# A graph-attention layer on one core: x loaded in 8 transfers of 128 partitions, four more adjacency pieces masked in halves

## The chip, the cores and the metric

One core of one Trainium2 chip runs the whole program. The metric is the device time of one execution in microseconds (us). TensorE multiplies matrices (PE; its weight loads are PEld), VectorE is DVE, ScalarE is ACT, GpSimd is POOL, and SyncE (SP) only issues transfers. ACT issues transfers too, in line with its own instructions. All transfers run on the core's 16 DMA engines.

## The reference

N = 4096 nodes with D = 128 features and a dense 4096 x 4096 int32 adjacency (67.1 MB; x is 2.1 MB):

```
s_i = emb @ attn[:d]
s_j = emb @ attn[d:]
e = leaky_relu(s_i + s_j.T, negative_slope=0.2)
e = e + where(adj > 0, 0.0, neg_inf)
alpha = softmax(e, axis=1)
x = layernorm(x + alpha @ emb, axis=-1)
```

## The kernel before

The rows are cut into 8 blocks of 512 (BLOCKS) and the columns into 4 pieces of 1024 (PIECES), which makes 32 adjacency pieces of 2 MB. ORDER interleaves the first two blocks and then goes block by block. Below, piece g is the g-th of this order; "pieces 5 to 8" are g = 5 to 8 with counting from 0. A piece is 8 chunks of 128 columns.

**Start.** SP loads the attention row (one row of 1 KB). Then x comes in three parts (X_CUTS): chunks 0 to 7, 8 to 15 and 16 to 31. Each part is four transfers, one for each quadrant of 32 partitions; SP issues the two low quadrants, ACT the two high ones. In the same queues the adjacency follows: pieces 0 and 1 by half rows (load_rows, 256 KB a transfer), the later ones by quadrants (load_piece, 512 KB). PE transposes x (turn_x), ACT copies the result out of PSUM (L407), PE multiplies it with the first half of attn for the row scores (s_i_piece, L884). DVE multiplies x with the second half (product_of, L611) and sums over features (sum_products, L607); ACT sums one of the four stripes (L416). DVE takes the largest s_j (L647, row_max_ready), PE spreads it over the partitions (L900), DVE reduces it again (L649), and exponentials of the scores follow on ACT (L421 to L428). Only then can the first weights be made. ACT's program has, in this order: its x loads, four transfers of piece 0, the copy of x tile 0, two transfers of piece 1, tiles 1 and 2, two more, tiles 3 and 4, L416, one transfer of piece 2, tiles 5 to 7, another, and then the exponentials.

**Steady state.** For each piece ACT turns the int32 adjacency into bytes: in halves for g in HALVED (half_to_bytes, L451, two instructions), else at once (to_bytes, L457). DVE transposes the bytes by 32 x 32 blocks into mask_t: in halves (turn_half, L679) or whole (turn, L666). It then makes one weight tile a chunk (weigh, L771), 8 a piece. PE accumulates xj times weights (block_product, L919, two passes a chunk); after each block it transposes the sums back (L913), and the last block goes the other way round (L924). DVE's program places the transpose of the next piece (or of its first half) after chunk TURN_AT = 5, or after chunk 7 for the pieces in LATE_TURNS; the second half of a halved piece is transposed after its chunk 3. At chunk 3 of pieces 9 and 10, DVE also does the residual of blocks 0 and 1.

Instructions of one engine run in the order of its program; there is no scheduler.

Of the kernel before, what the change touches and what calls it, by code (L numbers as in the profile page):

```python
# [14 lines left out]
def gat_kernel(nc: bass.Bass, x: bass.AP, adj: bass.AP, attn: bass.AP, out: bass.AP):  # L15
# [8 lines left out]
    P = 128  # L24
    N, D = x.shape
    DEN = D - 1
    Q = 4
    B = 32
    K = 4
    F = N // (Q * B * K)  # L30
# [21 lines left out]
    W_SLOTS = 12  # L52
    BY_DVE = 1
    SECOND_HALF_AT = 3
    HALVED = (0, 1, 2, 3, 4)
    TURN_AT = 5
    LATE_TURN_AT = PC - 1
    TURN_BACK_AT = 6
# [11 lines left out]
    BY_POOL = range(1, PC)  # L70
    SPLIT = (0, 1)
    ROWS_HALF = (slice(0, Q // 2), slice(Q // 2, Q))
    LATE_TURNS = (0, 1, 2)
    SLOPE = 0.2
    EPS = 1e-5
    NEG_INF = -1e9
# [11 lines left out]
    BACK_BANK = [1, 0]  # L88
    X_CUTS = [0, SC, 2 * SC, CHUNKS]
    X_PARTS = len(X_CUTS) - 1  # L90
    IN_FLIGHT = 3
    WARM = 14

    adj_v = adj.rearrange("(r f b k) (q u c) -> f u q b k r c", r=Q, f=F, b=B, k=K, q=Q, u=PIECES)
    x_v = x.rearrange("(q f b k) d -> q b f (k d)", q=Q, f=F, b=B, k=K)
    out_v = out.rearrange("(q f b k) d -> f q b (k d)", q=Q, f=F, b=B, k=K)
    xi_v = x.rearrange("(t p) d -> p t d", p=P)

    with ExitStack() as ctx:
# [156 lines left out]

            return x_raw[:, t, :]

        def load_x(queue, quadrants, part):

            first, stop = X_CUTS[part], X_CUTS[part + 1]
            for q in quadrants:
                queue.dma_start(x_raw[B * q:B * (q + 1), first:stop, :].rearrange("b (f k) d -> b f (k d)", k=K),  # L263
                                x_v[q, :, first // K:stop // K, :]).then_inc(x_loaded[part], 16)

        def load_piece(queue, quadrants, g):

# [43 lines left out]
        @block.sync  # L311
        def _(sp):

            sp.dma_start(attn_row_in[:], attn[:, :].rearrange("d o -> o d")).then_inc(attn_loaded, 16)
            for part in range(X_PARTS):
                load_x(sp, LOW_HALF, part)
            for g in SPLIT:
                for h in range(2):
                    load_rows(sp, LOW_HALF, g, h)
            for g in range(len(SPLIT), ALL_PIECES):  # L320
                load_piece(sp, LOW_HALF, g)


            for g in range(EARLY):
                sp.wait_ge(early_out_ready, g + 1)
                for q in LOW_HALF:
                    store_last(sp, g, q, last_stored)
            for g in range(EARLY, len(FINAL_GROUPS)):
                sp.wait_ge(last_out_ready, g - EARLY + 1)
                for q in LOW_HALF:  # L330
                    store_last(sp, g, q, last_stored)


            sp.wait_ge(again_ready, 1)
            with sp.If(sp.value_load(again[0:1, 0:1], min_val=0, max_val=1) > 0):
                sp.wait_ge(stored, 16 * Q * NORM_GROUPS)
                sp.wait_ge(early_stored, 16 * len(HIGH_HALF) * EARLY)
                sp.wait_ge(last_stored, 16 * (Q * len(FINAL_GROUPS) - len(HIGH_HALF) * EARLY))
                sp.dma_start(xi[:], xi_v).then_inc(inputs_again, 16)
                sp.dma_start(attn_col, attn[D:2 * D, :]).then_inc(inputs_again, 16)  # L340
                sp.dma_start(attn_row, attn[0:D, :].rearrange("d o -> o d").broadcast_to([P, D])).then_inc(inputs_again, 16)
                with sp.Fori(0, TILES) as t:
                    sp.wait_ge(adj_rows_free, t + 1)
                    sp.dma_start(adj_rows, adj[bass.ds(t * P, P), :]).then_inc(adj_rows_loaded, 16)
            sp.wait_ge(early_stored, 16 * len(HIGH_HALF) * EARLY)
            sp.wait_ge(last_stored, 16 * (Q * len(FINAL_GROUPS) - len(HIGH_HALF) * EARLY))
# [51 lines left out]
        @block.scalar  # L398
        def _(act):

            for part in range(X_PARTS):
                load_x(act, HIGH_HALF, part)
            for h in range(2):
                load_rows(act, HIGH_HALF, 0, h)
            for m in range(RB):
# [196 lines left out]
        def _(dve):  # L602
# [11 lines left out]
            def first_quarter(h):  # L614

                part = slice(0, P)
                nc.vector.tensor_scalar(mask_bytes[:, 0, :, ROWS_HALF[h], part], split_rows(0, h)[:, :, :, part], 0.0, None,  # L617
                                        ALU.is_gt).then_inc(half_bytes_ready, 1)
                dve.wait_ge(half_bytes_ready, h + 1)
                src = mask_bytes[:, 0, :, ROWS_HALF[h], part].bitcast(u32)  # L620
                dst = mask_t[:, 0, 0, :, :].rearrange("p i k -> p (i k)").bitcast(u32)
# [7 lines left out]
            dve.wait_ge(attn_i_in_psum, 1)  # L629
            nc.vector.tensor_copy(attn_iw[:], banks[ATTN_I_BANK][:, 0:P]).then_inc(attn_wide, 1)  # L630
            dve.wait_ge(attn_j_ready, 1)
            dve.wait_ge(x_loaded[0], 16 * Q)
            product_of(0)
            sum_products(0)
            dve.wait_ge(x_loaded[1], 16 * Q)
            product_of(1)
            sum_products(1)
            dve.wait_ge(x_loaded[2], 16 * Q)
            product_of(2)
            product_of(3)  # L640
            sum_products(3)
# [3 lines left out]
            dve.wait_ge(s_j_ready, STRIPES - 1)  # L645
            dve.wait_ge(s_j_by_act_ready, 1)
            nc.vector.reduce_max(smax[:, 0:1], s_j[:], X).then_inc(row_max_ready, 1)  # L647
            dve.wait_ge(max_spread, 1)
            nc.vector.reduce_max(smax[:, 1:2], banks[MAX_BANK][:, 0:P], X).then_inc(max_found, 1)  # L649
            dve.wait_ge(max_found, 1)  # L650
# [1 line left out]
            nc.vector.tensor_scalar(smax[:, 2:3], smax[:, 1:2], SLOPE - 1, None, ALU.mult).then_inc(max_scaled, 1)  # L652
            dve.wait_ge(adj_loaded[0], 16 * Q)
            first_quarter(1)

            def turn(g):

# [197 lines left out]
        def _(pe):  # L855
# [10 lines left out]
            def turn_x(m):  # L866

                if m * K in X_CUTS:
                    pe.wait_ge(x_loaded[X_CUTS.index(m * K)], 16 * Q)
                if m >= 4:  # L870
                    pe.wait_ge(xT_ready, m - 3)
                for k in range(K):
# [162 lines left out]
```

## Time and profile before

| | us |
|---|---|
| median of 3 runs (252.03 to 252.84) | 252.11 |
| the profiled execution | 252.82 |
| its span on the core | 251.0 |
| PE busy | 240.3 |
| DVE busy | 234.0 |
| ACT busy | 173.6 |

The profiled execution is 0.71 us above the median, and 1.8 us of it lie outside the span. PE's granted clock was full over the whole span. A busy PE means that a matmul was in flight: passes of 128x512 start every 0.43 us when nothing holds them.

### The profile page before, as it was taken

How to read it: one execution, taken by the hardware profiler on the slowest of the kernel's cores; microseconds unless marked ns; L12 is line 12 of the kernel's file. 1: busy time of each engine (PE TensorE's matmuls, PEld its weight loads, DVE VectorE, ACT ScalarE, POOL GpSimd, SP SyncE). 2: the span in 40 equal slices, each digit the busy share in tenths (PEclk: the TensorE clock that was granted, in tenths of full speed). 3: DMA queues.
4: the chain of work that ended last, by engine and by line, in shares of the span. 5: the costliest groups of instructions: out<-in, count | busy, mean ns of one | idle time of the engine just before them, and what ended most of it. 6: DMA issues, size and time to landing. Idle time of an engine off the chain costs nothing.

```text
span 251.0 us, 2790 instructions
## 1 busy us (share of the span) xinstructions
PE 240.3 (96%) x801; PEld 126.3 (50%) x801; DVE 234.0 (93%) x385; ACT 173.6 (69%) x253; POOL 42.9 (17%) x81
## 2 busy tenths in 40 slices
PE   7789999989999999999999999999999999999991
PEld 6444444334444444444444444444444444799991
DVE  1989999989999999999999999999999999999834
ACT  0688768889887696996996669686976559404402
POOL 1029000000000024430430003300330004300612
PEclk9999999999999999999999999999999999999999
DMA  7999999999999999999999999999999990100001
GB/s 198 299 346 347 350 348 347 348 347 347 347 347 349 345 349 348 336 359 351 347 349 363 347 348 347 347 363 347 350 347 363 347 281 3 44 0 1 24 21 45
DMA packets 70386, 71.50 MB, mean 285 GB/s; under 512 B 3009, under 2 KB 68866, under 8 KB 70370
## 3 DMA queue, kind: packets, MB, share of 16 engines
q1 hardware_dynamic: 34754, 34.74, 44.2%
q10 hardware_dynamic: 34656, 34.67, 43.9%
q0 software_dynamic: 960, 1.90, 2.4%
q8 instruction: 7, 0.11, 0.2%
q14 instruction: 9, 0.07, 0.1%
HBM read 69.21 MB, written 2.10 MB: 284 GB/s over the span
## 4 chain that ended last, share of the span: by engine, by line
PE 77%; DMA 14%; DVE 3%; ACT 2%; issue 1%; SPq 1%; ACTq 0%
PE psum L919 64%; PE psum L924 11%; DMA adj_in<-in_adj_dram 11%; DMA x_raw<-in_x_dram 3%; ACT mask_bytes L457 1%; PE psum L913 1%; DVE adj_in L611 1%; SPq L263 1%; ACT mask_bytes L446 1%; DVE s_j L607 0%; DVE weights L771 0%; DVE mask_bytes L617 0%; ACTq L282 0%; PE psum L900 0%; ACT q_row L428 0%
## 5 line engine op out<-in xcount | busy, mean ns | idle before, releaser
L919 PE MATMUL psum<-weights,xj 128*128 128x512 f32 x448 | 193.9, 593 | 1.5 <-DVE weights L771 1.5
L771 DVE SCALAR_TENSOR_TENSOR weights<-q_row,r_j,mask_t 128x512 f32<-128x512 f32 x256 | 172.5, 741 | 0.5
L919 PEld LDWEIGHTS psum<-weights,xj 128*128 128x128 f32 x448 | 84.5, 190 | 106.5 <-issue 82.2
L457 ACT ACTIVATE mask_bytes<-adj_in 128x4096 uint8<-128x4096 int32 x27 | 97.5, 3613 | 26.3 <-DMA adj_in<-in_adj_dram 22.6
L666 DVE STREAM_TRANSPOSE mask_t<-mask_bytes 128x1024 uint32<-128x1024 uint32 x27 | 33.4, 1236 | 1.0 <-ACT mask_bytes L457 1.0
L924 PEld LDWEIGHTS psum<-xj,weights 128*128 128x128 f32 x256 | 28.8, 192 | 0.5 <-issue 0.5
L924 PE MATMUL psum<-xj,weights 128*128 128x128 f32 x256 | 28.9, 275 | 0.0
L371 POOL TENSOR_SCALAR neg_mean<-total 128x4 f32<-128x4 f32 x7 | 2.1, 295 | 148.4 <-ACT x_raw L470 148.3
L380 POOL DMA_DIRECT2D out_dram<-x_raw x28 | 14.6, 527 | 19.7 <-ACT x_raw L484 19.6
L470 ACT ACTIVATE x_raw<-x_raw 128x128 f32<-128x128 f32 x28 | 8.2, 294 | 11.2 <-DVE x_raw L714 11.2
L451 ACT ACTIVATE mask_bytes<-adj_in 128x2048 uint8<-128x2048 int32 x6 | 11.1, 1902 | 4.4 <-DMA adj_in<-in_adj_dram 4.4
L477 ACT ACTIVATE unused<-x_raw,neg_mean 128x128 f32<-128x128 f32 x28 | 10.9, 390 | 4.3 <-POOL neg_mean L371 4.3
L484 ACT ACTIVATE x_raw<-x_raw,offset,rstd 128x128 f32<-128x128 f32 x28 | 11.5, 480 | 2.6 <-POOL offset L377 2.6
L434 ACT ACTIVATE xj<-x_raw,last_x,d_j 128x127 f32<-128x127 f32 x25 | 10.3, 479 | 0.0
L375 POOL TENSOR_TENSOR rstd<-variance,half 128x4 f32<-128x4 f32 x7 | 9.6, 1369 | 0.6
L714 DVE SCALAR_TENSOR_TENSOR x_raw<-psum,rden,x_raw 128x127 f32<-128x127 f32 x32 | 9.2, 344 | 0.4
L465 ACT COPY sums<-psum 128x512 f32<-128x512 f32 x7 | 4.1, 582 | 6.2 <-PE psum L919 6.2
L884 PE MATMUL psum<-adj_in,attn_iw 128*128 128x512 f32 x16 | 7.6, 597 | 0.4 <-ACT adj_in L407 0.4
L365 POOL TENSOR_SCALAR xj<-x_raw,d_j,last_x 128x127 f32<-128x127 f32 x7 | 7.0, 1010 | 0.1
L679 DVE STREAM_TRANSPOSE mask_t<-mask_bytes 128x512 uint32<-128x512 uint32 x9 | 6.3, 704 | 0.5 <-ACT mask_bytes L451 0.5
L446 ACT ACTIVATE mask_bytes<-adj_in 128x1024 uint8<-128x1024 int32 x6 | 5.9, 1046 | 1.2 <-DMA adj_in<-in_adj_dram 1.0
L554 ACT ACTIVATE deviations<-moments,eps 128x1 f32<-128x1 f32 x2 | 0.6, 295 | 8.4 <-DVE moments L738 8.4
(68 smaller groups left out, 85.0 us busy)
## 6 DMA issues: line engine op xcount, KB each, us to landing
adj_in<-in_adj_dram SPq DMA_DIRECT2D x60, 512.0 KB, 13.9
adj_in<-in_adj_dram ACTq DMA_DIRECT2D x60, 512.0 KB, 14.0
adj_in<-in_adj_dram ACTq DMA_DIRECT2D x8, 256.0 KB, 10.6
adj_in<-in_adj_dram SPq DMA_DIRECT2D x8, 256.0 KB, 11.2
out_dram<-x_raw POOLq DMA_DIRECT2D x28, 64.0 KB, 5.3
x_raw<-in_x_dram ACTq DMA_DIRECT2D x4, 128.0 KB, 3.4
x_raw<-in_x_dram SPq DMA_DIRECT2D x4, 128.0 KB, 3.7
x_raw<-in_x_dram ACTq DMA_DIRECT2D x2, 256.0 KB, 6.1
```

The source lines that it names most:

```text
L375: nc.gpsimd.tensor_tensor(rstd[:, 0:K], variance[:, 0:K], half[:, 0:K], ALU.pow).then_inc(rstd_ready, 1)
L380: pool.dma_start(out_v[g, q, :, :], x_raw[B * q:B * (q + 1), g * K:(g + 1) * K, :].rearrange("b k d -> b (k d)")).then_inc(stored, 16)
L434: nc.scalar.activation(xj[:, c, 0:DEN], x_raw[:, c, 0:DEN], ACT.Identity, bias=last_x[:, c:c + 1], scale=d_j[:, c:c + 1]).then_inc(xj_scal ...
L451: half_bytes = nc.scalar.activation(mask_bytes[:, g % BYTE_SLOTS, :, :, part], adj_in[:, g % ADJ_SLOTS, :, :, part], ACT.Sign)
L457: nc.scalar.activation(mask_bytes[:, g % BYTE_SLOTS, :, :, :], adj_in[:, g % ADJ_SLOTS, :, :, :], ACT.Sign).then_inc(bytes_ready, 1)
L477: last = nc.scalar.activation(unused[:, k, :], tile(g * K + k), ACT.Square, bias=neg_mean[:, k:k + 1], accum_out=square_sum[:, k:k + 1])
L484: last = nc.scalar.activation(tile(g * K + k), tile(g * K + k), ACT.Identity, bias=offset[:, k:k + 1], scale=rstd[:, k:k + 1])
L666: nc.vector.transpose(dst.rearrange("p f (r a) -> p r f a", a=B), src).then_inc(mask_ready, 1)
L714: nc.vector.scalar_tensor_tensor(features, sums_of(n, t)[:, 0:DEN], rden[:, t:t + 1], features, ALU.mult, ALU.add).then_inc(y_ready, 1)
L771: nc.vector.scalar_tensor_tensor(weights[:, slot_of(g * PC + j), :], q_row[:, n * BANK:(n + 1) * BANK], r_j[:, c:c + 1], mask_t[:, g % MAS ...
L919: nc.tensor.matmul(banks[SUM_BANK[n % 2]][:, :], xj[:, c, :], weights[:, slot_of(g * PC + j), :], start=(c == 0), stop=(c == CHUNKS - 1)). ...
L924: return nc.tensor.matmul(banks[((BLOCKS - 1) * K + t) % 8][:, 0:D], weights[:, slot, t * P:(t + 1) * P], xj[:, c, :], start=(c == 0), sto ...
```

## The change

x comes in 8 transfers of 256 KB. Transfer f takes chunks 4f to 4f + 3 of all 128 partitions, one run of 2 KB for each partition; SP issues the odd f and ACT the even ones. In DRAM the rows of one f lie in four groups of 32 rows, one group for each quadrant, 512 KB apart: the new x_v has dimensions f, q (4), b (32), 512 elements. Part 0 of x is now two transfers, part 1 two, part 2 four (LOADS). HALVED takes in pieces 5 to 8, LATE_TURNS takes in piece 3, and the transposes of piece 0's first quarter come out of first_quarter into turn_first_quarter, the first of them behind the largest s_j.

```diff
-    HALVED = (0, 1, 2, 3, 4)
+    HALVED = tuple(range(9))
-    LATE_TURNS = (0, 1, 2)
+    LATE_TURNS = (0, 1, 2, 3)
+    LOADS = [(stop - first) // K for first, stop in zip(X_CUTS, X_CUTS[1:])]
-    x_v = x.rearrange("(q f b k) d -> q b f (k d)", q=Q, f=F, b=B, k=K)
+    x_v = x.rearrange("(q f b k) d -> f q b (k d)", q=Q, f=F, b=B, k=K)
-        def load_x(queue, quadrants, part):
-
-            first, stop = X_CUTS[part], X_CUTS[part + 1]
-            for q in quadrants:
-                queue.dma_start(x_raw[B * q:B * (q + 1), first:stop, :].rearrange("b (f k) d -> b f (k d)", k=K),
-                                x_v[q, :, first // K:stop // K, :]).then_inc(x_loaded[part], 16)
+        def load_x(queue, f):
+
+            part = max(i for i in range(X_PARTS) if X_CUTS[i] <= f * K)
+            queue.dma_start(x_raw[:, f * K:(f + 1) * K, :].rearrange("p k d -> p (k d)"),
+                            x_v[f, :, :, :]).then_inc(x_loaded[part], 16)
...
-            for part in range(X_PARTS):
-                load_x(sp, LOW_HALF, part)
+            for f in range(1, F, 2):
+                load_x(sp, f)
...
-            for part in range(X_PARTS):
-                load_x(act, HIGH_HALF, part)
+            for f in range(0, F, 2):
+                load_x(act, f)
...
+
+            def turn_first_quarter(h):
+
+                part = slice(0, P)
                 dve.wait_ge(half_bytes_ready, h + 1)
...
-            dve.wait_ge(x_loaded[0], 16 * Q)
+            dve.wait_ge(x_loaded[0], 16 * LOADS[0])
...
             nc.vector.reduce_max(smax[:, 0:1], s_j[:], X).then_inc(row_max_ready, 1)
+            turn_first_quarter(0)
...
             first_quarter(1)
+            turn_first_quarter(1)
```

The first place is the head of SP's program; the sizes are those of the SBUF side (partitions, runs, elements of a run). On ACT the x rows change in the same way.

```order
 L311 UNCONDITIONAL_BRANCH
 L314 DMA attn_row_in<-in_L_gnn_attn_dram 1x256
-L263 DMA x_raw<-in_x_dram 32x2x512 x4
-L263 DMA x_raw<-in_x_dram 32x4x512 x2
+L263 DMA x_raw<-in_x_dram 128x1x512 x4
 L293 DMA adj_in<-in_adj_dram 32x8x256 x8
 L282 DMA adj_in<-in_adj_dram 32x16x256 x60
```

Six transfers became four on each queue, and the SBUF side of each now has 128 partitions with one run.

The second place is on DVE between the sums over features and the first weights; first before, then with the change.

```order
L607 TENSOR_REDUCE s_j<-adj_in 128x8
L617 TENSOR_SCALAR mask_bytes<-adj_in 128x4x2x128
L622 STREAM_TRANSPOSE mask_t<-mask_bytes 128x4x64
L647 TENSOR_REDUCE smax<-s_j 128x1
L649 TENSOR_REDUCE smax<-psum 128x1
L651 TENSOR_SCALAR below_max<-s_j,smax 128x32
```

```order
L607 TENSOR_REDUCE s_j<-adj_in 128x8
L617 TENSOR_SCALAR mask_bytes<-adj_in 128x4x2x128
L651 TENSOR_REDUCE smax<-s_j 128x1
L626 STREAM_TRANSPOSE mask_t<-mask_bytes 128x4x64
L654 TENSOR_REDUCE smax<-psum 128x1
L656 TENSOR_SCALAR below_max<-s_j,smax 128x32
```

One transpose moved behind the first of the two reductions to the largest s_j. Lines of the change are 4 to 6 higher.

The third place is on DVE from the weights of piece 3 (its second half) into piece 5; first before, then with the change.

```order
L771 SCALAR_TENSOR_TENSOR weights<-q_row,r_j,mask_t 128x512 x2
L679 STREAM_TRANSPOSE mask_t<-mask_bytes 128x512
L771 SCALAR_TENSOR_TENSOR weights<-q_row,r_j,mask_t 128x512 x6
L679 STREAM_TRANSPOSE mask_t<-mask_bytes 128x512
L771 SCALAR_TENSOR_TENSOR weights<-q_row,r_j,mask_t 128x512 x2
L666 STREAM_TRANSPOSE mask_t<-mask_bytes 128x16x2x32
L771 SCALAR_TENSOR_TENSOR weights<-q_row,r_j,mask_t 128x512 x8
```

```order
L777 SCALAR_TENSOR_TENSOR weights<-q_row,r_j,mask_t 128x512 x4
L685 STREAM_TRANSPOSE mask_t<-mask_bytes 128x512
L777 SCALAR_TENSOR_TENSOR weights<-q_row,r_j,mask_t 128x512 x4
L685 STREAM_TRANSPOSE mask_t<-mask_bytes 128x512
L777 SCALAR_TENSOR_TENSOR weights<-q_row,r_j,mask_t 128x512 x2
L685 STREAM_TRANSPOSE mask_t<-mask_bytes 128x512
L777 SCALAR_TENSOR_TENSOR weights<-q_row,r_j,mask_t 128x512 x6
L685 STREAM_TRANSPOSE mask_t<-mask_bytes 128x512
```

The first half of piece 4 is transposed two weights later, and piece 5 is transposed in two halves instead of at once.

## Rows read from the trace of the kernel before

**Rows 1.** The chain that ended last: start us, us, what.

```profile
3.41 7.58 DMA x_raw<-in_x_dram
...
83.61 27.47 PE psum L919 x64
```

**Rows 2.** Timeline of PE's products: start us, us, instructions, idle before.

```profile
19.59 25.91 PE L919 MATMUL psum<-weights,xj 128*128 128x512 f32 x60
45.85 7.13 PE L919 MATMUL psum<-weights,xj 128*128 128x512 f32 x16 [0.35 <-DVE weights L771]
54.17 16.12 PE L919 MATMUL psum<-weights,xj 128*128 128x512 f32 x37 [1.18 <-DVE weights L771]
```

**Rows 3.** Timeline of DVE at the start.

```profile
11.01 2.36 DVE L611 TENSOR_TENSOR adj_in<-x_raw,attn_j 128x1024 f32<-128x1024 f32 x2 [0.51 <-DMA x_raw<-in_x_dram]
...
15.26 0.45 DVE L622 STREAM_TRANSPOSE mask_t<-mask_bytes 128x256 uint32<-128x256 uint32 x1
...
17.07 0.69 DVE L617 TENSOR_SCALAR mask_bytes<-adj_in 128x1024 uint8<-128x1024 int32 x1
...
18.36 2.96 DVE L771 SCALAR_TENSOR_TENSOR weights<-q_row,r_j,mask_t 128x512 f32<-128x512 f32 x4
```

**Rows 4.** DMA issues: line, queue, count, KB each, median us from issue to landing.

```profile
x_raw<-in_x_dram ACTq DMA_DIRECT2D x4, 128.0 KB, 3.4
x_raw<-in_x_dram SPq DMA_DIRECT2D x4, 128.0 KB, 3.7
x_raw<-in_x_dram ACTq DMA_DIRECT2D x2, 256.0 KB, 6.1
x_raw<-in_x_dram SPq DMA_DIRECT2D x2, 256.0 KB, 6.9
...
attn_row_in<-in_L_gnn_attn_dram SPq DMA_DIRECT2D x1, 1.0 KB
```

**Rows 5.** Stretches; after the engines: granted clock, share of 16 DMA engines, GB/s.

```profile
2.00:9.00 7.00, 5.81 (x34) 4.90 (x34) 3.75 (x5) 2.30 (x4) 0.00 (x0) 1.00 1.02 278
...
20.00:24.00 4.00, 4.00 (x11) 1.81 (x10) 3.96 (x6) 3.01 (x4) 4.00 (x5) 1.00 1.10 348
```

**Rows 6.** The page's GB/s in 40 slices of 6.3 us.

```profile
GB/s 198 299 346 347 350 348 347 348 347 347 347 347 349 345 349 348 336 359 351 347 349 363 347 348 347 347 363 347 350 347 363 347 281 3 44 0 1 24 21 45
```

**Rows 7.** Issues of transfers: timeline, then piece 0 and 1's, ns min/median/max.

```profile
0.73 2.80 ACTq L263 DMA_DIRECT2D x_raw<-in_x_dram  x6
1.14 2.70 SPq L263 DMA_DIRECT2D x_raw<-in_x_dram  x6
...
L293 SPq DMA_DIRECT2D adj_in<-in_adj_dram x8: 622/738/1861, 3.9 to 10.2; - x8
```

**Rows 8.** Timeline of ACT at the start.

```profile
13.91 1.32 ACTq L282 DMA_DIRECT2D adj_in<-in_adj_dram  x1
...
14.63 1.52 ACT L407 COPY adj_in<-psum 128x512 f32<-128x512 f32 x3
...
16.96 0.23 ACT L421 ACTIVATE d_j<-below_max 128x32 f32<-128x32 f32 x1 [0.81 <-DVE below_max L651]
```

**Rows 9.** Timeline of DVE from 25 us on.

```profile
25.50 2.74 DVE L771 SCALAR_TENSOR_TENSOR weights<-q_row,r_j,mask_t 128x512 f32<-128x512 f32 x4
...
32.29 2.74 DVE L771 SCALAR_TENSOR_TENSOR weights<-q_row,r_j,mask_t 128x512 f32<-128x512 f32 x4
...
44.45 0.71 DVE L679 STREAM_TRANSPOSE mask_t<-mask_bytes 128x512 uint32<-128x512 uint32 x1 [0.48 <-ACT mask_bytes L451]
...
52.14 1.25 DVE L666 STREAM_TRANSPOSE mask_t<-mask_bytes 128x1024 uint32<-128x1024 uint32 x1 [0.96 <-ACT mask_bytes L457]
53.31 5.35 DVE L771 SCALAR_TENSOR_TENSOR weights<-q_row,r_j,mask_t 128x512 f32<-128x512 f32 x8
...
59.74 5.35 DVE L771 SCALAR_TENSOR_TENSOR weights<-q_row,r_j,mask_t 128x512 f32<-128x512 f32 x8
...
94.89 5.35 DVE L771 SCALAR_TENSOR_TENSOR weights<-q_row,r_j,mask_t 128x512 f32<-128x512 f32 x8
```

More of the change, by code:

```diff
@@ L631, in _ @@
             dve.wait_ge(attn_j_ready, 1)
-            dve.wait_ge(x_loaded[0], 16 * Q)
+            dve.wait_ge(x_loaded[0], 16 * LOADS[0])
             product_of(0)
             sum_products(0)
-            dve.wait_ge(x_loaded[1], 16 * Q)
+            dve.wait_ge(x_loaded[1], 16 * LOADS[1])
             product_of(1)
             sum_products(1)
-            dve.wait_ge(x_loaded[2], 16 * Q)
+            dve.wait_ge(x_loaded[2], 16 * LOADS[2])
             product_of(2)
@@ L868, in turn_x @@
                 if m * K in X_CUTS:
-                    pe.wait_ge(x_loaded[X_CUTS.index(m * K)], 16 * Q)
+                    pe.wait_ge(x_loaded[X_CUTS.index(m * K)], 16 * LOADS[X_CUTS.index(m * K)])
                 if m >= 4:
```

## The prediction

> **What bounds the kernel now.** I read the chain that ended last first. It starts with the transfer of x, which lands at 10.99 us, goes through DVE's products, and from there to the end is nearly all PE products [rows 1]. So I asked where PE itself stands still. Its products begin at 19.59 us and run at 27.47 / 64 = 0.429 us a pass [rows 1, 2]. The profile finds only two stops of PE after that, 0.35 and 1.18 us, both for DVE's weights [rows 2]. Whatever is to be gained or lost must therefore be a shift of 19.59, or those 1.5 us.
>
> Next the start. DVE's program is a chain of products and sums; x holds it up for only 0.51 us, at the last two stripes [rows 3]. The first weights begin at 18.36, right behind piece 0's second byte half (17.07 + 0.69) and its transpose [rows 3]. In the steady state the 16 DMA engines are full and deliver 348 GB/s [rows 5], so pieces of 2 MB come every 6.0 us, while PE takes 16 x 0.429 = 6.87 us for one. The adjacency is needed at its own pace only in the first pieces.
>
> **Part 1: x in 8 transfers.** Fewer issues save sequencer time only: two issues less on each queue at 2.80 / 6 = 0.47 us [rows 7], hidden because the engines are already full from 2 us on (share 1.02) [rows 5]. What matters is how a transfer is dealt to the 16 engines. All x and adjacency transfers of before have 32 rows outermost on the SBUF side and 32 or 128 on the DRAM side, and they fill all 16 engines [rows 5]. The one transfer with a single row, that of attn, is the only one in the view of issues without a time to landing [rows 4]: it did not end in 16 parts. So the number of parts follows the pattern. In the new transfer the SBUF side has 128 rows, but the DRAM side is 4 groups of 32 rows, since a quadrant's rows lie 512 KB from the next quadrant's, and no row of before shows such a shape. If the dealing goes by the outermost loop of both sides, only 4 of the 16 engines carry x. If it goes by runs or by SBUF rows, all 16 do.
>
> I take the first. Nothing in the rows shows the DRAM side of a transfer being cut below its outermost loop, and the outermost loops of before are all multiples of 16 except the one that shows no landing. The Trainium skill (DMA: Bandwidth & Descriptors, "Why a DMA increments its semaphore by 16 and not by 1") states this as a rule: the engines used are the largest number up to 16 that divides the slowest dimension, other than 1, of both patterns; here that is the largest divisor of 4 and 128, so 4. The attn row agrees with it, and no run here shows a 4 yet.
>
> The price: x is 2048 KB [rows 4], so each of the 4 engines carries 524,288 bytes. The highest rate that the page shows is 363 GB/s [rows 6], 22.7 GB/s for each engine, which gives 23.1 us. While x loads today the rate is 278 GB/s [rows 5], 17.4 per engine, which gives 30.2 us; that is the slow bound, with all 16 in each other's way. An engine whose neighbours are idle may go faster than 22.7, since that figure is shared among 16; I allow a tenth (an estimate) and get 20.8 us as the fast bound. I take 23.1, nearest to four engines alone. Traffic is full from 2.0 us [rows 5], so the last of x lands at 25.1 instead of 10.99: **+14.1 us**. The first adjacency pieces are queued behind x on these 4 engines, and a piece is complete only with all of its parts: piece 0 follows 131,072 / 22.7 = 5.8 us after x, at 30.9, where it came 6.1 us after x before (17.07). So adjacency moves with x, and at 5.8 to 6.0 us a piece it then keeps the pace it had.
>
> The Trainium skill also gives about 27 GiB/s for one engine (same page, "Specifications"). By it x would take 18.1 us and the whole sum be 5.0 us lower; no row here shows such a rate.
>
> **What the full queue does to ACT.** The issue of a 256 KB adjacency transfer takes 0.6 to 0.75 us at first and 1.86 at most [rows 7]: by 8 us the queues are full. SP had then issued 1 MB of x and 1.6 MB of adjacency, and half of 278 GB/s x 6.3 us, 0.9 MB, had left its queue: about 1.7 MB or some 105 runs of 1 KB for each engine is what a queue holds. With x on 4 engines a queue carries 4 x 32 = 128 runs on each of them, full as soon as x is issued. Each adjacency transfer then needs 16 free places, and gets them only as the 4 engines clear x, two queues sharing them: 16 x 2048 / 11.35 = 2.9 us. ACT issues eight of these among its copies of tiles 0 to 2, 8 x 2.9 = 23 us from about 2.6, so it reaches tile 3 at 25.8, 0.7 us after x. Then two transfers of piece 2 with 32 runs of 1 KB each, also 2.9 us apiece, stand between L416 and the exponentials, where today they take 0.6 and 1.3 us [rows 8]. Today the last copies end at 14.63 + 1.52 = 16.15, 5.2 us after x, and the exponentials start at 16.96, 6.0 after x [rows 8]. Late by 0.7 to 1.8 us, these partly hide behind PE's eight score passes, which end at 19.6, 8.6 after x.
>
> **Part 2: the transpose behind the largest s_j.** It takes 0.45 us [rows 3] out of the way of row_max_ready and lies then under PE's spread of the maximum. Worth at most 0.45, and nothing where DVE waits for piece 0 anyway. The delay on ACT and this gain go together: between -0.45 and +1.4; I take **+0.3**.
>
> **Part 3: halves for pieces 5 to 8, late turn of piece 4.** The late turn comes two weights (1.4 us) later than where DVE stands 0.48 us for ACT's bytes [rows 9]: that wait goes. The wait of 0.96 at piece 5 [rows 9] is for a whole L457 of 3.6 us; half of it is ready 1.7 us sooner, so it goes too. PE's two stops of 1.53 us end with them. But a halved piece costs DVE 32.29 - 25.50 = 6.79 us, a whole one 59.74 - 53.31 = 6.43 [rows 9]: 4 x 0.36 = 1.44 us more. DVE is hardly faster than PE's 6.87 in that stretch, so its lead must carry this until pieces 9 and 10 with their residuals. Today the weights for chunk 0 of piece 11, the third of the row at 94.89, end at 94.89 + 3 x 0.67 = 96.9 [rows 9], and PE takes them at 83.61 + 17 x 0.858 = 98.2 [rows 1]: lead 1.3. In the tight stretch the lead is (19.59 + 8 x 0.858) - (25.50 + 0.69) = 0.26 [rows 2, 9], and PE runs without a stop on it. DVE saves 1.44 of waits and pays 1.44 of halves, so PE can gain no more than the spare lead, 1.3 - 0.26, here rounded down: **-0.9 us** (bounds 0 and -1.5).
>
> **Sum.** 252.82 (the profiled execution) + 14.1 + 0.3 - 0.9 = 266.3; that execution is 0.71 above the median of 252.11, so 265.6 against the median. I say 265.5.
>
> **Rivals.** (a) *Same mechanism, slower*: x on 4 engines at today's 17.4 GB/s lands at 32.2, 21.2 later than now: 252.1 + 21.2 + 0.3 - 0.9 = 272.7, and 274.7 with ACT's blocked issues at their bound of 1.4 and nothing from part 3. Against it speaks that the rate of today is one that 16 engines share.
>
> (b) *Faster*: x is dealt to all 16 engines, by its 128 SBUF rows. Then x lands no later than now, and the start gains at most DVE's wait of 0.51 [rows 3], while DVE's first weights still wait for piece 0 at 17.07, whose bytes are no sooner there. What is left is part 3: 252.1 - 0.9 = 251.2 (250.7 to 251.7). For it speaks that today's transfers, whose runs are also 2 KB, fill all engines; against it, that none of them has fewer than 32 in its outermost loop. The point that decides is the number of engines: 14 or more at 17.4 GB/s bring x by 11 us. The Trainium skill ("Rules for kernel authors", same page) speaks for this side in advising one transfer of 128 partitions over two of half of them; its rule above has the condition that this shape fails.
>
> (c) *No change*: as (b), but DVE's 1.44 us of halves eat the lead up to piece 11 and PE stops there instead of at pieces 3 and 5: 252.1.
>
> **Chances.** Forecast (x on 4 engines, 261 to 269) 0.67; (a) 0.17; (b) 0.11; (c) 0.05. A change within 0.3%, 0.75 us, can't be told from none here. Slower 0.84, same 0.05, faster 0.11. The case of 4 engines has its own range: fast bound 252.1 + 14.1 - 2.3 - 0.45 - 1.5 = 261.9, slow bound 274.7; I give 261 to 274. The cases (b) and (c), 0.16, stay outside.
>
> **What would show it.** The x rows of the issues lose their time to landing, as attn's has none. The share of the DMA engines falls well under 1 in the first 20 us. DVE's last products (L611) start at about 25 instead of 11.01, PE's first product at about 34. SP's and ACT's issues of pieces 0 and 1 take about 2.9 us each. PE's stops at pieces 3 and 5 are gone, and the lead at piece 11 is near 0.3. The prediction is wrong if x lands at 11 us or before; then (b) or (c) holds.

## The result and the profile after

| | us | ratio to the kernel before (95% interval) |
|---|---|---|
| kernel before, median of 6 runs | 252.16 | |
| changed kernel, median of 6 runs (374.36 to 379.25) | 377.47 | 1.495 (1.4911 to 1.4989) |
| forecast | 265.5 (261 to 274) | 1.053 |

Slower was right, and the size was not: 125 us instead of 13. The profiled execution took 374.36 us, with a span of 372.6 where the one of before had 251.0: 121.6 us to find.

The chain of the changed kernel that ended last (start us, us, what) answers to [rows 1].

```profile
3.52 29.29 DMA x_raw<-in_x_dram
...
37.54 24.07 DMA adj_in<-in_adj_dram
...
61.63 0.02 ACT mask_bytes L451
...
61.69 18.68 DMA adj_in<-in_adj_dram
...
80.46 19.16 DMA adj_in<-in_adj_dram
...
329.30 3.62 ACT mask_bytes L457
...
342.74 24.53 PE psum L930 x200
```

It begins, as forecast, with a late x: 3.52 + 29.29 = 32.81 us instead of 10.99. But then it does not become PE's products. It is adjacency, transfer after transfer, up to 329 us. Each link is about 19 us and carries the chain on by two pieces.

The page of the changed kernel: the GB/s in 40 slices (9.3 us each), the count of packets, the chain by engine, one group of instructions, and the issues of x.

```profile
GB/s 69 176 157 212 224 220 213 216 216 217 216 216 217 217 216 216 216 217 226 236 215 213 216 254 215 216 217 236 242 212 217 252 239 218 225 90 28 1 30 30
DMA packets 70226, 71.50 MB, mean 192 GB/s; under 512 B 2849, under 2 KB 68706, under 8 KB 70210
...
DMA 86%; PE 7%; ACT 4%; issue 1%; ACTq 1%; DVE 1%; POOL 0%
...
L457 ACT ACTIVATE mask_bytes<-adj_in 128x4096 uint8<-128x4096 int32 x23 | 83.2, 3617 | 101.5 <-DMA adj_in<-in_adj_dram 101.5
...
x_raw<-in_x_dram ACTq DMA_DIRECT2D x4, 256.0 KB
x_raw<-in_x_dram SPq DMA_DIRECT2D x4, 256.0 KB
```

The slices that read 336 to 363 in [rows 6], mostly near 348, read 212 to 254 here, mostly near 216, from the fourth slice to the end of the adjacency. ACT stands 101.5 us waiting for it ahead of L457. The x rows have lost the time to landing that they had in [rows 4]. I read this as for the attn row: the transfer doesn't end in 16 parts. The pages' counts of small packets bear it out, if each part ends with one. Under 512 B the page of before counts 3009 packets and this one 2849: 160 fewer, and 12 x 16 - 8 x 4 is 160.

Stretches of the changed kernel (length; busy time and instructions of PE, PEld, DVE, ACT, POOL; granted clock, DMA share, GB/s), beside [rows 5]. The last row is the kernel before in the same 100 us.

```profile
5.00:10.00 5.00, 0.93 (x4) 0.63 (x3) 0.58 (x2) 0.00 (x0) 0.00 (x0) 1.00 0.26 102
10.00:20.00 10.00, 3.55 (x16) 3.14 (x16) 4.01 (x4) 0.25 (x1) 0.00 (x0) 1.00 0.65 170
...
60.00:160.00 100.00, 80.90 (x173) 33.12 (x172) 68.32 (x109) 53.90 (x62) 2.17 (x4) 0.93 1.11 216
...
60.00:160.00 100.00, 100.00 (x246) 45.08 (x246) 99.72 (x161) 79.80 (x106) 16.84 (x30) 1.00 1.10 349
```

Two things are to be seen. While x loads, the share is 0.26, which is 4.2 of 16 engines, and these move 102 GB/s. From 60 us on the engines are busy all the time (1.11, before: 1.10) and yet move only 216 GB/s, where the kernel before has 349. A full share alone is no proof of a full rate.

The timelines of PE and of DVE in the changed kernel, beside [rows 2] and [rows 3].

```profile
44.24 7.12 PE L925 MATMUL psum<-weights,xj 128*128 128x512 f32 x16 [2.20 <-issue]
54.33 10.17 PE L925 MATMUL psum<-weights,xj 128*128 128x512 f32 x16 [2.97 <-DVE weights L777]
65.22 4.96 PE L925 MATMUL psum<-weights,xj 128*128 128x512 f32 x11 [0.72 <-DVE weights L777]
```

```profile
32.83 2.36 DVE L611 TENSOR_TENSOR adj_in<-x_raw,attn_j 128x1024 f32<-128x1024 f32 x2 [11.95 <-DMA x_raw<-in_x_dram]
...
42.01 0.79 DVE L617 TENSOR_SCALAR mask_bytes<-adj_in 128x1024 uint8<-128x1024 int32 x1 [2.74 <-DMA adj_in<-in_adj_dram]
```

**Where the 121.6 us are.** Before, PE came to piece 2 at 19.59 + 2 x 6.87 = 33.3 us [rows 1, 2]; now at 65.22: 31.9 late. From piece 2 (bytes at 61.63) to piece 30 (329.30) a piece takes (329.30 - 61.63) / 28 = 9.56 us instead of PE's 6.87: 28 x 2.69 = 75.3 more. The remainder, 14.4, is behind the last pieces, whose bytes, sums and normalization no longer lie under PE's products. So not quite a fifth is x (21.8 us at its landing), and most of the rest is the rate of the adjacency; with that rate restored, in e11 below, the time is 269.28 us.

### The profile page after: what moved, and what is told of

The parts are those of the page before. It is cut to its first block, busy times and chain, and to the rows that moved or that the text cites. A ratio compares the mean times of both kernels' runs of the same rounds, so it can differ in the third digit from the quotient of the medians.

```text
span 372.6 us, 2795 instructions
## 1 busy us (share of the span) xinstructions
PE 275.1 (74%) x801; PEld 138.9 (37%) x801; DVE 238.6 (64%) x389; ACT 174.5 (47%) x257; POOL 37.5 (10%) x81
## 2 busy tenths in 40 slices
DMA packets 70226, 71.50 MB, mean 192 GB/s; under 512 B 2849, under 2 KB 68706, under 8 KB 70210
## 3 DMA queue, kind: packets, MB, share of 16 engines
q10 hardware_dynamic: 34576, 34.67, 46.9%
## 4 chain that ended last, share of the span: by engine, by line
DMA 86%; PE 7%; ACT 4%; issue 1%; ACTq 1%; DVE 1%; POOL 0%
DMA adj_in<-in_adj_dram 78%; DMA x_raw<-in_x_dram 8%; PE psum L930 7%; ACT mask_bytes L457 2%; ACTq L263 1%; ACT adj_in L416 1%; ACT x_raw L484 0%; ACT unused L477 0%; ACT adj_in L407 0%; ACT x_raw L470 0%; PE psum L879 0%; PE psum L919 0%; ACT sums L465 0%; DVE x_raw L752 0%; DVE x_raw L720 0%
## 5 line engine op out<-in xcount | busy, mean ns | idle before, releaser
L925 PE MATMUL psum<-weights,xj 128*128 128x512 f32 x448 | 216.8, 641 | 36.5 <-DVE weights L777 34.2
L925 PEld LDWEIGHTS psum<-weights,xj 128*128 128x128 f32 x448 | 89.7, 206 | 158.3 <-issue 98.1
L457 ACT ACTIVATE mask_bytes<-adj_in 128x4096 uint8<-128x4096 int32 x23 | 83.2, 3617 | 101.5 <-DMA adj_in<-in_adj_dram 101.5
L672 DVE STREAM_TRANSPOSE mask_t<-mask_bytes 128x1024 uint32<-128x1024 uint32 x23 | 28.6, 1244 | 50.4 <-ACT mask_bytes L457 50.4
L451 ACT ACTIVATE mask_bytes<-adj_in 128x2048 uint8<-128x2048 int32 x14 | 26.0, 1903 | 30.7 <-DMA adj_in<-in_adj_dram 30.7
L919 PE MATMUL psum<-ident,sums 128*128 128x128 f32 x28 | 7.2, 408 | 35.5 <-ACT sums L465 35.5
L685 DVE STREAM_TRANSPOSE mask_t<-mask_bytes 128x512 uint32<-128x512 uint32 x17 | 12.0, 708 | 25.0 <-ACT mask_bytes L451 21.8
L919 PEld LDWEIGHTS psum<-ident,sums 128*128 128x128 f32 x28 | 5.0, 208 | 41.4 <-ACT sums L465 39.8
L611 DVE TENSOR_TENSOR adj_in<-x_raw,attn_j 128x1024 f32<-128x1024 f32 x4 | 4.8, 1224 | 21.6 <-DMA x_raw<-in_x_dram 21.6
L879 PE MATMUL psum<-ident,x_raw 128*128 128x128 f32 x32 | 7.1, 394 | 13.1 <-DMA x_raw<-in_x_dram 13.1
L879 PEld LDWEIGHTS psum<-ident,x_raw 128*128 128x128 f32 x32 | 5.9, 210 | 16.5 <-DMA x_raw<-in_x_dram 15.3
```

The source lines that it names most:

```text
L451: half_bytes = nc.scalar.activation(mask_bytes[:, g % BYTE_SLOTS, :, :, part], adj_in[:, g % ADJ_SLOTS, :, :, part], ACT.Sign)
L457: nc.scalar.activation(mask_bytes[:, g % BYTE_SLOTS, :, :, :], adj_in[:, g % ADJ_SLOTS, :, :, :], ACT.Sign).then_inc(bytes_ready, 1)
L672: nc.vector.transpose(dst.rearrange("p f (r a) -> p r f a", a=B), src).then_inc(mask_ready, 1)
L685: nc.vector.transpose(dst.rearrange("p (r a) -> p r a", a=B), src).then_inc(mask_ready if f else half_mask_ready, 1)
L879: last = nc.tensor.transpose(banks[XT_BANK + m % 4][:, k * P:(k + 1) * P], x_raw[:, m * K + k, :], ident[:])
L919: last = nc.tensor.transpose(banks[BACK_BANK[n % 2]][:, t * P:(t + 1) * P], sums[:, t * P:(t + 1) * P], ident[:])
```

## The experiments

The theory that I formed from these rows, P: (1) x goes over 4 engines, because the DRAM side has 4 groups outermost; (2) these four fall behind the other twelve, and with that the two queues fall out of step; (3) SP's queue writes only partitions 0 to 63 and ACT's only 64 to 127, and transfers into one half of the partitions reach some 217 GB/s. The rivals: the four engines' lag costs the rate by itself; part 3 or the order of DVE does it; the DRAM side is what is shared.

One thing has to be kept in mind throughout. A quadrant of the partitions always receives the same quarter of the adjacency's columns (q stands for both in adj_v). So "one half" below means 64 partitions and, in DRAM, the half of the columns that goes into them.

**e1: of the change only x; e2: all but x.**

e1 is the kernel before with this, e2 the changed kernel without it:

```diff
+    LOADS = [(stop - first) // K for first, stop in zip(X_CUTS, X_CUTS[1:])]
-    x_v = x.rearrange("(q f b k) d -> q b f (k d)", q=Q, f=F, b=B, k=K)
+    x_v = x.rearrange("(q f b k) d -> f q b (k d)", q=Q, f=F, b=B, k=K)
...
-                load_x(sp, LOW_HALF, part)
+            for f in range(1, F, 2):
+                load_x(sp, f)
...
```

> The kernel before with the x loads of the change and nothing else. Theory A (the x transfers alone cost the 125 us; the halves and the moved transposes are worth about a microsecond): 373 to 381 us, x landing near 33 us, adjacency at about 217 GB/s to the end. Theory B (the x transfers cost what their own landing is late, about 22 us, and the more frequent byte instructions and issues of the halved pieces on ACT slow the rest): 270 to 280 us and 340 GB/s or more.

> The change with the x loads of before: what is left is pieces 5 to 8 in halves, the late turn of piece 4 and the transpose behind the largest s_j. Theory A, with the prediction's own part 3: 0.9 us less than before (bounds 0 and 1.5), so 251.2, with PE's stops at pieces 3 and 5 gone and the lead of DVE at piece 11 near 0.3 us. Theory B: 345 us or more, as the slow adjacency would come from this part.

Measured: e1 376.15 us, ratio 1.491 (1.4879 to 1.4941); e2 251.19 us against 252.33, ratio 0.9955 (0.9943 to 0.9967). All of the loss is x's, and the rest of the change alone is worth 1.1 us. PE's timeline in e2:

```profile
19.06 54.45 PE L925 MATMUL psum<-weights,xj 128*128 128x512 f32 x126
...
94.70 14.86 PE L925 MATMUL psum<-weights,xj 128*128 128x512 f32 x34 [0.47 <-DVE weights L777]
```

The first products come 0.53 us earlier than in [rows 2], the two stops there (1.53 us) are gone, and a new one of 0.47 stands at 94.70, at chunk 6 of piece 10: 0.53 + 1.53 - 0.47 = 1.6, and the spans differ by 251.0 - 249.5 = 1.5.

**e3: the kernel before, with both queues in the same half of the partitions at a time** (x is dealt as before).

```diff
-    LOW_HALF = (0, 1)
-    HIGH_HALF = (2, 3)
+    LOW_HALF = (0, 2)
+    HIGH_HALF = (1, 3)
```

> The kernel before with another share of the quadrants: SP moves quadrants 0 and 2, ACT 1 and 3, so that in step both queues write into the same 64 partitions, and x and the adjacency are dealt to 16 engines as before. Theory P (the rate of about 217 GB/s is what one half of the partitions takes, and the change is slow because its two queues take turns): the adjacency falls to 217 to 260 GB/s and the time rises to 310 to 378 us. Theory D (the rate comes from the DRAM side, from engines that read out of step, or from the number of runs): 250 to 256 us, since all engines read in step as before.

Measured: 358.17 us, ratio 1.4197 (1.4122 to 1.4273). The stretch from 60 to 160 us in e3:

```profile
60.00:160.00 100.00, 79.04 (x170) 33.16 (x171) 68.24 (x105) 56.68 (x73) 8.49 (x16) 0.91 1.12 219
```

219 GB/s at a full share, with no transfer on 4 engines at all: that both queues are in one half is enough for the rate. The lag of the four engines is not needed for it; it can only be what brings the queues into this state.

**e5: the same, crossed**: SP takes quadrants 0 and 2, ACT 3 and 1, so that each queue changes halves but the two are in different ones while they keep step.

```diff
-    LOW_HALF = (0, 1)
-    HIGH_HALF = (2, 3)
+    LOW_HALF = (0, 2)
+    HIGH_HALF = (3, 1)
```

> The kernel before with SP moving quadrants 0, then 2, and ACT quadrants 3, then 1: each queue still changes halves, as where both queues wrote into the same 64 partitions, but in step the two are now in different halves. Theory P (two queues in the same half of the partitions share what one half takes): 250 to 262 us and about 345 GB/s, as long as the queues stay in step; a queue that is one transfer ahead would put both into one half again, which its landings would show. Theory Q (a queue that changes halves from transfer to transfer is slow whatever the other one does, or the DRAM side is): 340 us or more.

Measured: 271.45 us, ratio 1.0765 (1.071 to 1.082). The stretch in e5:

```profile
60.00:160.00 100.00, 97.42 (x236) 42.84 (x237) 96.87 (x156) 71.72 (x89) 13.72 (x24) 1.00 1.11 313
```

Against e3 only ACT's order differs, and the rate goes from 219 to 313. So what counts is which quadrants the two queues move at the same time. That doesn't yet say on which side: with the partitions, the columns that are read at the same time have changed too. And 313 isn't the 345 that P expected, nor 271 us its 250 to 262; whether the queues slip now and then in e5 I have not settled.

**e4: the changed kernel, with the adjacency issued only when all of x has landed.**

```diff
+            for part in range(X_PARTS):
+                sp.wait_ge(x_loaded[part], 16 * LOADS[part])
...
+            for part in range(X_PARTS):
+                act.wait_ge(x_loaded[part], 16 * LOADS[part])
```

> The change, with both queues waiting until all of x has landed before they issue any adjacency. x still goes over 4 engines. Theory P with the four engines' lag as the cause (adjacency queued behind x leaves these 4 engines behind the other 12, and the queues then never fall into step): no lag arises, x lands at about 23 to 25 us, the adjacency runs at 345 GB/s or more, and the time is 264 to 272 us. If the slow adjacency has another cause that lasts (something that the x transfers leave in the queues or in the DRAM rows): 216 GB/s again and 380 us or more.

Measured: 272.98 us, ratio 1.082 (1.0801 to 1.084), 1 us above the range that P expected. Stretches, SP's issues and PE's products in e4:

```profile
10.00:20.00 10.00, 3.93 (x16) 3.13 (x16) 4.89 (x4) 0.00 (x0) 0.00 (x0) 1.00 0.26 102
...
40.00:100.00 60.00, 60.00 (x144) 26.71 (x143) 59.47 (x89) 52.06 (x55) 6.38 (x6) 1.00 1.10 348
```

```profile
24.52 5.48 SPq L293 DMA_DIRECT2D adj_in<-in_adj_dram  x8
```

```profile
41.22 34.07 PE L929 MATMUL psum<-weights,xj 128*128 128x512 f32 x79
```

With the four engines to itself x moves at 102 GB/s, which is 25.5 for each engine; by that its 524,288 bytes an engine take 20.6 us. SP's first adjacency issue, which waits for x, starts at 24.52. And with x on four engines but nothing behind it, the adjacency has its 348 GB/s. So the lost rate isn't x's shape in itself; it takes adjacency that is issued behind x while four engines are late.

**e6: the changed kernel with one pause**: piece 8 is issued only when piece 7 has landed.

```diff
-                landed = g - IN_FLIGHT
+                landed = g - (1 if g == 8 else IN_FLIGHT)
```

> The change, with one pause: piece 8 of the adjacency is issued only when piece 7 has landed whole (instead of piece 5), and from there on as before. ACT stands still in its program for that, which costs perhaps 10 us once. Theory L (the four engines stay behind by the x they carried, and as long as they are behind, each of the other twelve has work from one queue at a time): 216 GB/s until piece 7 lands at about 110 us, 345 GB/s from then on, PE then sets the pace with 6.87 us a piece: 295 to 315 us. Rival (the slow rate does not need the lag, it would come back by itself): 216 GB/s again after the pause and 375 us or more.

Measured: 302.6 us, ratio 1.2 (1.1965 to 1.2035). Stretches of e6 before, in and after the pause:

```profile
60.00:80.00 20.00, 15.38 (x32) 6.26 (x31) 13.62 (x20) 10.49 (x12) 0.00 (x0) 0.91 1.11 214
...
100.00:110.00 10.00, 4.84 (x11) 1.78 (x10) 3.06 (x5) 6.53 (x10) 0.00 (x0) 0.93 0.65 146
...
120.00:130.00 10.00, 10.00 (x28) 4.67 (x27) 9.96 (x16) 8.59 (x6) 0.00 (x0) 1.00 1.10 348
...
140.00:200.00 60.00, 60.00 (x147) 26.93 (x146) 59.79 (x99) 48.10 (x63) 13.93 (x23) 1.00 1.10 351
```

One pause takes the rate from 214 to 348, and it stays there. The slow pace is a state that the start leaves behind, not a property of the transfers that run in it. That it keeps itself up until a pause is shown; how it does so is not.

**The queues themselves.** The load of the two queues (packets, MB, share of 16 engines) in two windows of the changed kernel, 104 to 107 and 109 to 112 us, q10 and q1 being the two that carry the adjacency:

```profile
q10 hardware_dynamic: 556, 0.55, 98.8%
q1 hardware_dynamic: 78, 0.08, 13.8%
...
q1 hardware_dynamic: 555, 0.56, 98.1%
q10 hardware_dynamic: 81, 0.08, 13.9%
```

The same in the kernel before, 107 to 110 us:

```profile
q10 hardware_dynamic: 519, 0.52, 55.0%
q1 hardware_dynamic: 521, 0.52, 54.2%
```

And in e3, 104 to 107 us:

```profile
q10 hardware_dynamic: 329, 0.32, 56.5%
q1 hardware_dynamic: 327, 0.32, 55.6%
```

Before, both queues share the engines evenly. In the changed kernel one has nearly all of them, and 5 us later the other. In e3 the queues are in step and the rate is low all the same, since in step they write one half. What all slow windows have in common is the half. The smaller queue's 78 of 634 packets are about two engines' worth of sixteen. That would fit four engines which serve both queues in turn while twelve serve one; which engine carried a packet the views don't show, so this is an inference.

**e7: the changed kernel, with the DRAM side of x as 128 rows.**

```diff
-    x_v = x.rearrange("(q f b k) d -> f q b (k d)", q=Q, f=F, b=B, k=K)
+    x_v = x.rearrange("(f p k) d -> f p (k d)", f=F, p=P, k=K)
```

> The change, but each x transfer reads 128 rows of 2 KB that follow each other in DRAM, so that the DRAM side has 128 rows outermost instead of 4 groups of 32. The SBUF side, the size and the number of the transfers, and both queues are those of the change. This loads the rows of x in another order, so the output is that of a permuted x. Theory A (the engines that a transfer uses follow the outermost loop of both of its sides): 16 engines, x lands by 11 us, 345 GB/s, 250 to 253 us. Rival (it is the shape of 128 partitions with one run each, or 8 transfers instead of 12): 370 us or more.

Measured: 250.72 us, ratio 0.9943 (0.9921 to 0.9965). The issues of x and the stretch of [rows 5] in e7:

```profile
x_raw<-in_x_dram ACTq DMA_DIRECT2D x4, 256.0 KB, 4.2
x_raw<-in_x_dram SPq DMA_DIRECT2D x4, 256.0 KB, 4.8
```

```profile
2.00:9.00 7.00, 7.00 (x33) 6.45 (x32) 3.29 (x5) 2.55 (x4) 0.00 (x0) 1.00 1.05 345
```

Size, partitions and issues are those of the change; only the DRAM side differs, 128 rows that follow each other instead of 4 groups of 32 that lie 512 KB apart. The time to landing is back, the share is full, and the 125 us are gone. The Trainium skill (DMA: Bandwidth & Descriptors, "Why a DMA increments its semaphore by 16 and not by 1") has the rule: the engine count is the largest number up to 16 that divides the slowest dimension, other than 1, of both sides. The 4.2 engines of the change and the full share of e7 agree with it, and so do e7's packets under 512 B: 2946, which is 63 fewer than before, where 12 x 16 - 8 x 16 would be 64. The attn row, which I had called in agreement, is no evidence for the rule: its one dimension other than 1 has 256 elements, which 16 divides, and yet its landing is missing.

**e9 and e10: the kernel before, with all adjacency issued by SP**; in e9 quadrant after quadrant, in e10 each transfer over all 128 partitions.

e9:

```diff
...
-                load_piece(sp, LOW_HALF, g)
+                load_piece(sp, range(Q), g)
...
-            load_piece(act, HIGH_HALF[0:1], 3)
...
```

e10 is e9 with:

```diff
-    adj_v = adj.rearrange("(r f b k) (q u c) -> f u q b k r c", r=Q, f=F, b=B, k=K, q=Q, u=PIECES)
+    adj_v = adj.rearrange("(f k p) (r u c) -> f u k p r c", f=F, k=K, p=P, r=Q, u=PIECES)
...
-                queue.dma_start(adj_in[B * q:B * (q + 1), g % ADJ_SLOTS, :, :, :],
-                                adj_v[n, p, q, :, :, :, :]).then_inc(adj_loaded[g % ADJ_SLOTS], 16)
+                queue.dma_start(adj_in[:, g % ADJ_SLOTS, q, :, :],
+                                adj_v[n, p, q, :, :, :]).then_inc(adj_loaded[g % ADJ_SLOTS], 16)
...
```

> The kernel before with all adjacency transfers issued by SP, quadrant after quadrant, on all 16 engines; x comes as before over both queues. At any time almost all writes go into one quadrant. Theory P (one half of the partitions takes about 217 GB/s): 217 to 230 GB/s and 345 to 380 us. Theory S (an engine with work from one queue alone is slower than with two): about the same. Theory D (the two queues disturb each other on the DRAM side when they are out of step): one queue can't, so 340 GB/s or more and 252 to 258 us.

> As the kernel with one queue, but each transfer fills all 128 partitions with 4 runs of 1 KB (2 in the half rows), so that its 16 engines write into both halves at once; size, runs and number of the transfers are the same. The mask comes from other places of the adjacency, so the output is that of a permuted adjacency. Theory P: 335 GB/s or more and 250 to 258 us, from one queue alone. Theory S: 217 to 240 GB/s as with one queue and quadrants, 340 us or more.

Measured: e9 362.14 us, 362.14 / 252.01 = 1.437 without an interval (a second run took 367.92, and the profile is that run's); e10 252.47 us, ratio 1.0014 (0.9998 to 1.0031). The stretch in e9, then in e10:

```profile
60.00:160.00 100.00, 78.43 (x164) 32.94 (x163) 66.40 (x103) 54.43 (x72) 8.51 (x16) 0.88 1.12 213
```

```profile
60.00:160.00 100.00, 100.00 (x247) 45.03 (x246) 99.72 (x161) 79.43 (x105) 18.03 (x32) 1.00 1.10 351
```

One queue brings 213 GB/s if it writes quadrant by quadrant and 351 if each transfer goes over all partitions. So one queue isn't too little in itself. The DRAM side differs here as well: an e10 transfer reads all four column quarters, an e9 transfer one.

**e11: the changed kernel, x still on its four engines, with e10's adjacency transfers on both queues.** The edit is e10's second diff, on the changed kernel.

> The change, with x still on its four engines, but each adjacency transfer of both queues fills all 128 partitions (four runs of 1 KB in each) where it filled one quadrant; the adjacency that reaches the masks is permuted by this, all work and sizes stay. Theory P (the four engines let the queues fall out of step, and it is only because each queue writes one half of the partitions that this halves the rate): x still lands late, at 24 to 33 us, its rows still show no time to landing, and the queues may still be out of step; but the adjacency then comes at 330 to 352 GB/s from 60 us on, PE runs without long stops, and the time is 262 to 277 us. Rival (the lag of the four engines itself costs the rate, whatever the partitions, since a piece is complete only with their parts): 60:160 stays at 210 to 240 GB/s and the time at 350 to 380 us.

Measured: 269.28 us, ratio 1.0669 (1.0643 to 1.0695). The stretch in e11, its queues from 104 to 107 and from 109 to 112 us, DVE's last products and PE's first:

```profile
60.00:160.00 100.00, 99.67 (x245) 44.73 (x244) 99.58 (x159) 82.35 (x103) 13.56 (x24) 1.00 1.08 347
```

```profile
q10 hardware_dynamic: 603, 0.60, 63.0%
q1 hardware_dynamic: 441, 0.45, 46.9%
...
q10 hardware_dynamic: 771, 0.77, 80.9%
q1 hardware_dynamic: 274, 0.27, 28.6%
```

```profile
28.08 2.36 DVE L611 TENSOR_TENSOR adj_in<-x_raw,attn_j 128x1024 f32<-128x1024 f32 x2 [9.23 <-DMA x_raw<-in_x_dram]
```

```profile
36.91 33.64 PE L925 MATMUL psum<-weights,xj 128*128 128x512 f32 x78
```

This run decides against the lag by itself. x is late here too, by its shape, though less than in the changed kernel (28.08 instead of 32.83), and the queues are out of step, though less far (63.0% against 46.9%, then 80.9% against 28.6%). The rate is 347 GB/s all the same. The rival, that the lag costs the rate whatever the partitions, wanted 210 to 240. With e10 the reading is that either queue alone now reaches both halves.

**What stays open** is the side. In every slow run a half of the partitions goes with a half of the columns, and e10 and e11 spread both at once, so no run tells SBUF from DRAM here. x, whose quadrants lie 512 KB apart in DRAM, doesn't settle it: its last two transfers on ACT land 7.3 us after their issue in e3 against 6.1 in [rows 4], but 7.2 in e5 too. A run with other columns in the same quadrants would tell.

**e8: e2 with only piece 5 added to HALVED**, the late turn kept.

```diff
-    HALVED = tuple(range(9))
+    HALVED = tuple(range(6))
```

> The x loads of before with the rest of the change, but halves only for pieces 0 to 5 instead of 0 to 8. The three pieces 6 to 8 cost DVE 3 x 0.36 = 1.1 us less. With halves to piece 8 PE stopped again at piece 10, for 0.5 to 0.8 us. Theory A (DVE's lead at pieces 10 and 11 is what the halves use up): no stop there, 250.2 to 250.7 us, 0.5 to 0.8 less than with halves to 8. Rival (whole pieces 6 and 7 come too late for DVE, which now runs earlier): PE stops at piece 6 or 7, and 251 us or more.

Measured: 251.44 us, ratio 0.9963 (0.9949 to 0.9977), against 0.9955 (0.9943 to 0.9967) for e2: the two can't be told apart. PE's and DVE's timelines in e8:

```profile
59.68 14.86 PE L925 MATMUL psum<-weights,xj 128*128 128x512 f32 x34 [0.43 <-DVE weights L777]
```

```profile
57.75 1.25 DVE L672 STREAM_TRANSPOSE mask_t<-mask_bytes 128x1024 uint32<-128x1024 uint32 x1 [0.37 <-ACT mask_bytes L457]
```

With fewer halves the stop moves from chunk 6 of piece 10 to chunk 6 of piece 5 (92 passes, two a chunk): there DVE first transposes piece 6, the first whole one, and waits 0.37 us for its L457. In the kernel before the second stop lies likewise at chunk 6 of piece 4 (60 + 16 passes), behind the transpose of piece 5. A stop of 0.43 to 0.47 is left either way.

## Why the prediction was wrong

**The step that failed** is the last of Part 1: "So adjacency moves with x, and at 5.8 to 6.0 us a piece it then keeps the pace it had". It came at 9.56 us a piece and never recovered, and that made 75 us of the 121.6 and, through the first and the last pieces, more. I took the 348 GB/s of [rows 5] for what 16 busy engines deliver. It is what they deliver when the two queues move different halves at the same time: 213 to 219 GB/s with one half (e3, e9), 347 to 351 with both (e10, e11), and x on four engines, with adjacency issued behind it, is enough to take the two queues apart (e4, e6). Nothing in the rows of before shows the slow pace, but the two queues' quadrants stood in the program, and a run on the kernel before (e3) would have shown the price.

The Trainium skill (SBUF — State Buffer, "Door 1: The DMA port swizzle (why `[64,N]` ≈ `[32,N]`)") has a rule that I had not weighed: a transfer's rate depends on how many of 16 ports its partitions reach, and partitions 0 to 63 reach one port of each pair, 64 to 127 the other. By its 435 GB/s for all 16, one half would have an estimated 217.5; the 213 to 219 of e3 and e9 and the 216 of the changed kernel agree. That the ports are what limits these runs is not shown apart from the columns.

**What was right.** x goes over 4 engines: 0.26 of 16, no time to landing, 160 small packets fewer, and e7 undoes it by the DRAM side alone. Slower was right for this reason, and rival (b), all 16 engines, is out for this kernel. With the one wrong step taken away (e11) the time is 269.28, inside the range of 261 to 274 that stood for the mechanism and 3.8 above the forecast; x is 3.0 us later there than I had it (28.08 against 25.1).

**Terms that were mis-sized.** x's landing, +14.1, measured +21.8 (32.81 against 10.99). Of an engine's rate I took 22.7 GB/s; with four engines alone it is 25.5 (e4), so that x takes 20.6 us, close to my fast bound of 20.8. The rest of the error goes the other way: x, which e4 has by 24.5, comes at 32.81 when adjacency is issued behind it, 8.3 us later. I had every piece strictly behind x; but from 10 to 20 us, with x still loading, 170 GB/s are moved where x alone makes 102, so adjacency is moved before x is through.

**ACT's full queue.** The issues take 26.12 / 8 = 3.3 us on SP where 2.9 was forecast (the last two rows are ACT's):

```profile
7.66 26.12 SPq L293 DMA_DIRECT2D adj_in<-in_adj_dram  x8
...
37.54 0.59 ACTq L282 DMA_DIRECT2D adj_in<-in_adj_dram  x1
39.25 0.23 ACT L421 ACTIVATE d_j<-below_max 128x32 f32<-128x32 f32 x1 [0.88 <-DVE below_max L656]
```

The two issues of piece 2 on ACT, for which I had 2.9 us each as well, took 0.59. On the path the full queue cost nothing at first: ACT's exponentials wait for DVE, as in [rows 8], and come 6.4 us after x, before 6.0. The first weights wait for the second half of piece 0, for which DVE stands 2.74 us until 42.01. I had piece 0 at 30.9.

**Part 3** was right in sign and size: in e2 PE's stops go from 1.53 to 0.47 us, 1.06 less, where I had 0.9. The lead is used up, as forecast (0.3 left at piece 11), and a little more: the stop of 0.47 stands two chunks earlier, at piece 10. What the transpose behind the largest s_j is worth (part 2) is not settled. PE's products start 0.53 us sooner in e2, but e8, whose program is the same up to there, starts them at 19.40, 0.19 sooner; no run tried the transpose alone.

**The list of what would show it.** Right: x's landing times missing, share under 1, about 3 us an issue, PE's two stops gone (in e2; in the changed kernel PE starves anyway). Wrong: DVE's last products at 32.83 instead of 25, PE's first at 44.24 instead of 34. No sign on the list looked at the pace of the adjacency behind x, the step that failed.

**The best version** is e2, 251.19 us: pieces 5 to 8 in halves and the late turn with x as it was, 1.1 us below the kernel before; e8 can't be told from it. e7 and e10 show rates, not versions: x or the adjacency is permuted in them.

## What to carry to other kernels

Before transfers are merged, look at the outermost loop of both sides: 4 groups in DRAM gave 4 engines, and the view of issues shows it by a missing time to landing, the windows by a share of 0.26. Where two queues each move one half of the partitions (here with one half of the columns), the full rate hangs on their keeping step; a burst on a few engines can part them for the rest of the run, as here. Two things helped: transfers that go over all 128 partitions and all column quarters (347 GB/s out of step), and one pause behind the burst (348 GB/s after it). And a bandwidth read from a trace holds for the pattern of transfers in that trace: ask what of the pattern the change takes away.

## What the runs showed of the hardware that I had not expected

- With all traffic in one half (64 partitions and their columns) the 16 engines move 213 to 219 GB/s while they show as fully busy (share 1.11 to 1.12); in both 347 to 351.
- One queue alone, issued by SP, delivers 351 GB/s (e10), as much as two.
- An engine with three quarters of its neighbours idle moves 25.5 GB/s in runs of 2 KB (102 / 4, e4), against 21.8 (348 / 16) when all are full with runs of 1 KB.
- The stretch from 2 to 9 us, in which x loads, delivers 345 GB/s in e7 against 278 before [rows 5]. In e7 both the partitions of a transfer and the order of its rows in DRAM differ; which of the two does it was not tried.
